# One masked write of Z in two 128-partition copies instead of four 16-partition copies

## The reference

```
x: layernorm, then q, k (64 per head) and v (128 per head) by projection,
   causal convolution of 4 taps, silu; q and k are normalised
for each token t:
   S = a_t * (S - b_t * k_t (k_t^T S)) + k_t v_t^T
   o_t = S^T q_t
o: rms norm, times Wo, layernorm, residual
then: token-shift feed-forward (sigmoid gate, squared relu), layernorm, residual
```

## Time and profile before

| | before |
|---|---|
| median of three runs | 3731.08 us |
| span of the profiled execution | 3725.1 us |
| busy: TensorE / its weight loads | 3292.6 / 2742.6 us (88% / 74%) |
| busy: VectorE, ScalarE, GpSimd | 2605.8, 2677.6, 2301.4 us (70%, 72%, 62%) |
| L941, 512 copies on VectorE | 146.6 us |
| mean granted TensorE clock | 0.922 |

### The profile page before, as it was taken

One profiled execution on the slowest core, in us unless ns is written; L12 is line 12 of the kernel. 1 busy time (PEld: TensorE's weight loads), 2 busy tenths in 40 slices (PEclk: granted clock), 3 DMA queues, 4 the chain that ended last, 5 costly groups with the idle time before them and its releaser, 6 DMA issues. The chain is left out here.

```text
span 3725.1 us, 195058 instructions
## 1 busy us (share of the span) xinstructions
PE 3292.6 (88%) x77978; PEld 2742.6 (74%) x77978; DVE 2605.8 (70%) x5465; ACT 2677.6 (72%) x5548; POOL 2301.4 (62%) x3558
## 2 busy tenths in 40 slices
PE   5699999999999999999999999999999999999775
PEld 4577777777777777777777777777777777777643
DVE  6677777777777777777777777777777777777453
ACT  2577777777777777777777777777777777777553
POOL 2456666666666666666666666666666666666345
PEclk9789999999999999999999999999999999999777
DMA  2223223232323232323323232323233232323111
GB/s 59 52 61 64 62 62 67 57 67 56 69 56 70 58 66 58 66 59 64 64 60 64 60 67 57 71 57 67 61 63 64 60 65 59 65 59 70 42 34 46
DMA packets 911057, 226.12 MB, mean 61 GB/s; under 512 B 820128, under 2 KB 894112, under 8 KB 911008
## 3 DMA queue, kind: packets, MB, share of 16 engines
q1 hardware_dynamic: 910848, 224.91, 28.8%
q0 software_dynamic: 160, 0.53, 0.0%
HBM read 169.73 MB, written 55.58 MB: 60 GB/s over the span
## 5 line engine op out<-in xcount | busy, mean ns | idle before, releaser
L852 DVE SCALAR_TENSOR_TENSOR cv<-ps,w_kq,cv 128x512 f32<-128x512 f32 x768 | 575.5, 749 | 417.1 <-ACT cv L719 403.5
L852 DVE SCALAR_TENSOR_TENSOR cv<-ps,w_v,cv 128x512 f32<-128x512 f32 x768 | 575.4, 749 | 153.0 <-ACT cv L719 134.9
L1016 POOL TENSOR_TENSOR accT<-accT,X 128x512 f32 (+1 forms) x128 | 163.3, 1276 | 530.2 <-ACT Y L817 530.2
L502 PE MATMUL ps<-xnT,w_kq 128*128 (+1 forms) x1024 | 325.7, 442 | 74.6 <-DVE cv L852 69.0
L502 PE MATMUL ps<-xnT,w_v 128*128 (+1 forms) x1024 | 335.2, 453 | 15.2 <-DVE cv L852 15.0
L1007 POOL TENSOR_TENSOR Sg<-S,tabR 128x512 f32<-128x512 f32 x256 | 333.8, 1323 | 0.0
L976 POOL TENSOR_TENSOR sc<-tabP,sc 128x8 f32<-128x8 f32 x128 | 26.3, 206 | 497.5 <-DVE sc L867 497.5
L765 ACT ACTIVATE Vt<-ps,sc 128x128 f32<-128x128 f32 x1024 | 278.8, 384 | 54.8 <-PE ps L571 54.8
L706 PE MATMUL ps<-wo_s,oo 128*128 128x128 f32 x2048 | 305.6, 309 | 1.2 <-issue 1.2
L967 POOL TENSOR_TENSOR Lm<-k_all,tabP 128x512 f32<-128x512 f32 x256 | 277.2, 1102 | 30.5 <-POOLq L182 30.5
L706 PEld LDWEIGHTS ps<-wo_s,oo 128*128 128x128 f32 x2048 | 280.8, 220 | 14.5 <-issue 1.7
(11 more groups left out here) (197 smaller groups left out, 8542.9 us busy)
## 6 DMA issues: line engine op xcount, KB each, us to landing
ex<-scrG SPq DMA_DIRECT2D x256, 128.0 KB, 2.9
scrN<-Nd SPq DMA_DIRECT2D x256, 128.0 KB, 2.6
Z<-scrZ SPq DMA_DIRECT2D x256, 128.0 KB, 3.2
X<-scrX SPq DMA_DIRECT2D x512, 64.0 KB
w_kq<-wtab SPq DMA_DIRECT2D x128, 132.0 KB, 2.2
w_v<-wtab SPq DMA_DIRECT2D x128, 132.0 KB, 2.5
wo_s<-wo SPq DMA_DIRECT2D x128, 128.0 KB, 2.8
NS<-scrN SPq DMA_DIRECT2D x128, 64.0 KB, 2.6
```

The source lines that it names most:

```text
L502: last = nc.tensor.matmul(pj[:, 4 * g:4 * g + 4, 0:CW], w[:, (j % 2) * P:(j % 2 + 1) * P], xnT3[:, 4 * g:4 * g + 4, bass.ds((n % NC) * C, ...
L852: nc.vector.scalar_tensor_tensor(cv4[:, j], pj[:, :, k:k + C], tap(j, k), cv4[:, j], ALU.mult, ALU.add).then_inc(conv[j].sem, 1)
```

## The change

The constant table `k_all` gets 64 more columns: a mask over [128 x 64] that is 1.0 where the first level's result belongs (16 rows x 16 columns in each 32x32 diagonal block) and 0.0 elsewhere. `dve_z0` no longer copies four rectangles of 16 partitions x (8 batches x 16 columns), one per group of 32 partitions. It issues two `copy_predicated`, one per PSUM bank, each over all 128 partitions and 4 batches x 64 columns = 256 elements per partition: where the mask, reread for each batch and taken as unsigned integers, is not zero, the product goes into Z, and Z stays as it was elsewhere. A `sem_inc` on a new semaphore `dve_go` stands between the wait and the first copy.

```diff
-K_N = K_XI + 272
+K_Z0 = K_XI + 272
+K_N = K_Z0 + 64
...
+    c[:, K_Z0:K_Z0 + C] = (r % 32 < 16) & (j // 32 == r // 32) & (j % 32 >= 16)
...
+        dve_go = sig("dve_go")
...
             dve.wait_ge(z_mm.sem, z_mm.at(m, 1))
-            zp = pair(PB["z0"]).rearrange("p g (b c) -> p g b c", b=4)
-            zs = two(half(BD["Z"], 0)).rearrange("p g (b c) -> p g b c", b=4)
-            for r in range(0, P, 32):
-                o = r % C
-                last = nc.vector.tensor_copy(zs[r:r + 16, :, :, o + 16:o + 32], zp[r:r + 16, :, :, o + 16:o + 32])
+            dve.sem_inc(dve_go.sem, 1)
+            mask = over(kc(K_Z0, C).bitcast(mybir.dt.uint32), 4, C)
+            for g in range(2):
+                last = nc.vector.copy_predicated(half(BD["Z"], 0)[:, g * 4 * C:(g + 1) * 4 * C].rearrange("p (b c) -> p b c", b=4), mask,
+                                                 bank(PB["z0"] + g)[:, 0:4 * C].rearrange("p (b c) -> p b c", b=4))
             last.then_inc(z_ok.sem, 1)
```

## The result

| | before | after |
|---|---|---|
| median of six runs each | 3731.70 us | 3743.01 us |
| range of the runs | 3730.17 to 3736.78 | 3737.72 to 3746.51 |
| ratio, with its 95% interval | | 1.0034 (1.0019 to 1.0048) |
| span of the profiled execution | 3725.1 us | 3740.1 us |
| mean granted TensorE clock | 0.922 | 0.916 |

The time lies in the stated range, but not in the case that was called likeliest: the loss is more than the 0.2% that counted as no change. The interval rests on six runs of each; in the 90 runs that the kernel before had beside the experiments it took from 3711.36 to 3743.84 us. Lines of the code after are three higher than before (L855 is L852 of before, L588 is L585).

A forecast was written before the change was run, and what follows sets the result against it. No engine is full, so the order of waits bounds the kernel. Span 3725.1 + 0 for the steps + 0.1 for mask columns = 3725.2, plus 6.0 to the runs' median: 3731.2 us; range 3718 to 3745, the forecast's own 3727 to 3736.

The forecast's parts named there:

- the stated range: Whole kernel: 3718 to 3745 us, meant to leave out no more than 2 in 10.
- the case that was called likeliest: Whole kernel: no change, 3731.2 us, within about 0.2% (7.5 us); chance 0.72.
- The price of the copies: VectorE's Z copies: each masked copy 421 ns, the overlapping pair 0.76 us, against 1.19 us for the four old copies.
- VectorE's busy sum falls by 40 us: VectorE over the whole run: busy sum 40 us lower (146.6 - 256 x 0.421 = 38.8), with the same span.
- L780 is held by ScalarE's own list: ScalarE: L780 follows tap 0 by its free distance, 0.58 to 0.63 us, so an earlier L585 does not move it.
- Sum for the 128 steps: 0: All steps together: 0 gained on the path, against a nominal 55 us of VectorE time.
- Effect on the path: TensorE's L585 and L595 start up to 0.29 us earlier in 92 steps; L780 stays, and TensorE idles 0.3 us longer before L533.
- the clock moves: Rival on TensorE's granted clock: half-clock stretches fall elsewhere, giving 3747 or 3715 us; chance 0.08 slower, 0.07 faster.
- a tenth of the loss: TensorE's clock: share of the 160 us lost to reduced clock assumed to be added or taken away, giving 3747 or 3715 us.
- 0.31 us to spare, point of decision 1.50 us for the pair: Tap 0 of k has 0.31 us free, so the masked pair slows the step only beyond 1.19 + 0.31 = 1.50 us.
- The `sem_inc` at 0 to 0.1 us: VectorE between wait and first copy: the added `sem_inc` costs 0 to 0.1 us.
- The mask columns at 0.1 us: First load: 32 KB more of mask columns cost 0.1 us once, bounds 0 to 0.2.

The follow-up runs named there:

- e3_half: Kernel before with only two of the four old copies (partitions 0 and 64), half of Z's first-level result missing: 3746.75 us, ratio 1.0040.
- e7_sem: Kernel before with only a `sem_inc` added between the wait and the four old copies: 3708.15 us, ratio 0.9954.
- e8_later: Kernel before with a `sem_inc` and then a 128x140 memset in front of the four old copies: 3735.26 us, ratio 1.0023.
- e6_cols: Kernel before with only the 64 unused mask columns added to the constant table: 3726.00 us, ratio 0.9998.
- e1_prep: Kernel before with the 64 unused mask columns and the `sem_inc`, old copies kept: 3704.86 us, ratio 0.9926.
- e11_masklate2: Changed kernel with a 128x556 memset on VectorE between the wait and the masked copies: 3705.83 us, ratio 0.9942.
- e2_delay: Changed kernel with a 128x400 memset on VectorE between the wait and the masked copies: 3734.59 us, ratio 1.0009.
- e5_masklate: Changed kernel with a 128x530 memset on VectorE between the wait and the masked copies: 3716.46 us, ratio 0.9965.

## Why the prediction was right and wrong

- *The price of the copies* was right: 440 ns against 421, the pair 0.77 against 0.76 us. They overlap: 0.77 is less than 2 x 0.44. That is what the rule cited in the prediction (the Trainium skill, VectorE: DVE Perf Modes, section Two Vector instructions with no wait between them) says of instructions that start at one partition, and the trace agrees. The forecast that VectorE's busy sum falls by 40 us left the overlap out: the copies' sum fell by 47, and with the prediction's own pair of 0.76 us it would have been 49.
- *L780 is held by ScalarE's own list* was right: L588 starts 0.28 us earlier against the k projection, L783 only 0.05 and it ends where it did, L536 waits 0.61 us instead of 0.33 (forecast 0.6), and L855 waits 1.33 instead of 1.04 (forecast 1.4). e3_half shows the same with other means: Z 0.6 us earlier, full-clock steps unchanged.
- *Sum for the 128 steps: 0* failed, and with it the 0.72 for no change. The step that failed is "Effect on the path": it counted only waits. TensorE's products L585 and L595 moved by 0.28 us in a pause, the full-clock step stayed at 25.2 us, and in the profiled executions seven steps out of 127 more were of the longest kind. The rival "the clock moves" named the place, the two groups that move 0.3 us, and the order of size, 16 us for a tenth of the loss (15.0 measured between the spans, 11.3 between the medians), but it was given only 0.08. A tenth was a round number, so its closeness is luck. That the time is in the stated range is owed to this rival: the range of the forecast itself ended at 3736. Its "against it" (work and step length remain) does not hold as an argument: in e3_half and e7_sem the work on TensorE and the full-clock step remained, and the clock moved all the same.
- *0.31 us to spare, point of decision 1.50 us for the pair* was wrong by a factor of three: 0.10 us was free, which puts that point at about 1.29 us for the pair. I took the slack of ScalarE's tap 0 and overlooked that TensorE needs 0.40 us around its loop's end. The idle 0.50 us before the k projection was put down to VectorE by the profile, and that was so, but only 0.10 of it was free. e8_later shows it: Z 0.2 us later costs 0.08 us per step.
- *The `sem_inc` at 0 to 0.1 us* was a little too low, 0.12. In the changed kernel Z is ready at 2031.17, 0.15 us before L588 starts, so nobody should be held up by it there, though no run leaves it out; in e7_sem it is the only edit, and the gain is 0.46%.
- *The mask columns at 0.1 us* cost nothing that can be measured (e6_cols).

Open remains why the granted clock answers to L585's place. The traces show the two orders of the kinds of step (mostly 1.00, 0.94, 0.94, 0.88 in the kernel before and after; 1.00, 0.94, 1.00, 0.94, 0.88, 0.94 in e7_sem), that the better one came with L585 3.57 us ahead of the k projection at an unchanged step length (e1_prep and e11_masklate2 have it too), and that half a microsecond less of TensorE's work per step did not bring it. They don't show what in the second level's place tips it.

The kernel that beats both is the one before with a `sem_inc` in front of its copies: 3704.86 us with the unused mask columns (e1_prep, ratio 0.9926) and 3708.15 without (e7_sem, 0.9954). The change itself comes out level with them, 3705.83 us (0.9942), with a memset that holds it back; its 47 us less of copying (146.6 to 99.2) bring nothing that can be measured here.

## What to carry to other kernels

When a program repeats a step whose length differs by the granted clock, first count the kinds of step before and after: if each kind kept its length, no wait on the path has changed, and the time went to the clock. Then look at more than one execution, since the counts scatter from run to run. Work that moves inside a pause is not always free; a delay of a tenth of a microsecond at the right place was worth 0.5 to 0.7% here, and an earlier start cost 0.3 to 0.4%. And before calling idle time slack, look for the floor below it: delay the instruction in front and see when the idle time stops shrinking.

## What the runs showed of the hardware

- A `copy_predicated` of 128x256 float32 from PSUM to SBUF with a mask in SBUF takes 440 ns; two of them without a wait between take 0.77 us. Behind a memset they took 405 ns each (e2_delay, e11_masklate2).
- A `sem_inc` between a wait and the instruction behind it cost VectorE 0.12 us (e7_sem: 0.20 us from the product's end to the copies, 0.08 before).
- At full clock TensorE's list needed 0.40 us from the last product of a loop body to the first of the next (e7_sem, e8_later); behind the last pass of the loop it was 0.06 us.
- The time followed the place of two product groups inside TensorE's pauses, at an unchanged full-clock step: ratios from 1.0040 to 0.9926 for leads from 4.04 to 3.57 us.
- The ranges of the runs differ between kernels: 3701.6 to 3710.2 us for e1_prep (6 runs), 3694.6 to 3728.4 for e5_masklate (12 runs). Whether that comes from a place between two orders of the kinds of step is not shown.
